# Two graph-attention layers on 128 small graphs: quads of graphs, layer by layer, unrolled, in place of pairs of graphs with both layers interleaved in a loop

## The reference

```python
# layer 0: attention, output projection, residual, norm
q = (x @ Wq + bq).reshape(b, n, H, HD)      # k and v likewise
scores = jnp.einsum('bqhd,bkhd->bhqk', q, k) / jnp.sqrt(jnp.float32(HD))
scores = scores + (1.0 - adj)[None, None, :, :] * -1000000000.0
attn = jax.nn.softmax(scores, axis=-1)
out = jnp.einsum('bhqk,bkhd->bqhd', attn, v).reshape(b, n, d)
x = _layernorm(x + (out @ Wo + bo))
# layer 1: the same with its own Wq, Wk, Wv, a mask where adj == 0, and no Wo
x = _layernorm(x + attention(x))
```

## Time and profile before

| what | value |
|---|---|
| median of 3 runs | 3196.25 us (3194.61 to 3197.16) |
| the profiled execution, its own time | 3195.59 us |
| its span, first to last instruction | 3193.8 us |
| PE, DVE, ACT, POOL busy | 98%, 63%, 53%, 36% of the span |
| granted TensorE clock, mean | 0.992 |
| HBM read, written | 75.11 MB, 33.55 MB |

### The profile page before, as it was taken

One profiled execution on the slowest core, in us unless ns is written; L12 is line 12 of the kernel. 1 busy time (PEld: TensorE's weight loads), 2 busy tenths in 40 slices (PEclk: granted clock), 3 DMA queues, 4 the chain that ended last, 5 costly groups with the idle time before them and its releaser, 6 DMA issues.

```text
span 3193.8 us, 78685 instructions
## 1 busy us (share of the span) xinstructions
PE 3121.4 (98%) x25100; PEld 2796.6 (88%) x25100; DVE 2007.7 (63%) x7062; ACT 1683.2 (53%) x5773; POOL 1157.1 (36%) x1093
## 2 busy tenths in 40 slices
PE   6999999999999999999999999999999999999994
PEld 6998898898888888988988888889889889888894
DVE  4566666666666666666666665666666666666654
ACT  4555555555555555555555555555555555555552
POOL 1333333333333333333333333333333333333332
PEclk9999999999999999999999999999999999999997
DMA  4333333333333333333333333333333333333332
GB/s 154 77 103 102 89 100 97 98 92 96 104 94 90 102 101 90 101 101 93 93 97 103 95 90 105 98 91 102 101 90 97 98 101 92 94 104 95 91 99 70
DMA packets 346121, 310.45 MB, mean 97 GB/s; under 512 B 38896, under 2 KB 301296, under 8 KB 346096
## 3 DMA queue, kind: packets, MB, share of 16 engines
q1 hardware_dynamic: 344800, 309.48, 36.6%
q10 hardware_dynamic: 1296, 0.67, 0.1%
HBM read 75.11 MB, written 33.55 MB: 34 GB/s over the span
## 4 chain that ended last, share of the span: by engine, by line
PE 80%; DVE 12%; issue 5%; DVEq 1%; DMA 0%; POOL 0%; ACT 0%; SPq 0%; POOLq 0%
PE ps_proj L371 41%; PE ps_proj L380 29%; PE ps_att L415 6%; PE ps_score L403 4%; DVE prob L778 4%; DVE x_res L869 2%; DVE x L809 2%; DVE stats L793 1%; DVE neg_max L778 1%; DVE xt_hi L741 1%; DVE mean_var L796 0%; DVE inv_sum L786 0%; DVEq L1004 0%; DMA prob<-w_q 0%; DVEq L775 0%
## 5 line engine op out<-in xcount | busy, mean ns | idle before, releaser
L1030 POOL TENSOR_TENSOR prob<-prob,inv_sum 128x512 f32<-128x512 f32 x512 | 525.5, 1042 | 1153.4 <-DVE inv_sum L786 1153.4
L597 ACT ACTIVATE prob<-prob,neg_max 128x128 f32<-128x128 f32 x2048 | 792.8, 391 | 261.3 <-DVE neg_max L778 261.2
L371 PE MATMUL ps_proj<-xt_hi,w_hi_q 128*128 128x256 f32 x2048 | 593.7, 290 | 32.3 <-ACT xt_hi L607 14.3
L371 PE MATMUL ps_proj<-xt_hi,w_lo_q 128*128 128x256 f32 x2048 | 580.6, 283 | 0.0
L371 PE MATMUL ps_proj<-xt_lo,w_hi_q 128*128 128x256 f32 x2048 | 580.4, 283 | 0.0
L371 PE MATMUL ps_proj<-xt_hi,w_hi_k 128*128 128x256 f32 x2048 | 579.7, 283 | 0.0
L371 PE MATMUL ps_proj<-xt_lo,w_hi_k 128*128 128x256 f32 x2048 | 579.6, 283 | 0.0
L371 PE MATMUL ps_proj<-xt_hi,w_lo_k 128*128 128x256 f32 x2048 | 579.3, 283 | 0.0
L778 DVE CUSTOM_DVE_ANT_0 prob<-ps_score,mask 128x128 f32<-128x128 f32 x2048 | 459.5, 283 | 16.5 <-PE ps_score L403 4.8
L819 DVE STREAM_TRANSPOSE blocks_t<-prob 128x512 f32<-128x512 f32 x512 | 341.7, 696 | 200.4 <-DMA prob_t<-blocks_t 164.3
L371 PEld LDWEIGHTS ps_proj<-xt_hi,w_hi_q 128*128 128x128 f32 x2048 | 392.7, 192 | 56.8 <-DVE x_res L869 17.8
(11 more groups left out here) (78 smaller groups left out, 4996.6 us busy)
## 6 DMA issues: line engine op xcount, KB each, us to landing
prob_t<-blocks_t SPq DMA_DIRECT2D x1024, 128.0 KB, 2.7
y<-x_feat SPq DMA_DIRECT2D x128, 256.0 KB, 2.6
x_res<-x_tok SPq DMA_DIRECT2D x64, 512.0 KB, 3.6
prob_t<-prob SPq DMA_DIRECT2D x512, 64.0 KB, 2.1
out<-y SPq DMA_DIRECT2D x128, 256.0 KB, 2.0
prob_t<-blocks_t SPq DMA_DIRECT2D x256, 64.0 KB, 2.1
y<-y SPq DMA_DIRECT2D x256, 64.0 KB, 2.1
prob<-w_q SPq DMA_DIRECT2D x2, 512.0 KB, 7.0
```

What stands on the lines that cost most here:

```text
L371: last = pe.matmul(ps_out[:, i * T:(i + 1) * T], wp[:, c, cols], xp[:, c, :], start=(c == 0 and n == 0), stop=(c == NC - 1 and n == 2))
L597: last = act.activation(prob[b][:, i, n, :], prob[b][:, i, n, :], ACT.Exp, bias=neg_max[l][b][:, i, n:n + 1], scale=-1.0, accum_out=row_su ...
L1030: pool.tensor_tensor(prob[b][:, i], prob[b][:, i], inv_sum[l][b][:, i, :].unsqueeze(2).to_broadcast([P, HB, NODES]), ALU.mult).then_inc(no ...
```

## The change

The program becomes layer by layer. A step takes a quad of graphs (QB = 4, T = 512 tokens); steps 0 to 31 are layer 0, steps 32 to 63 layer 1, and step 64 finishes. In a step PE projects quad s and, between these units, finishes the attention of quad s-1. q and k are projected with 512 columns a matmul (`feature_unit`, L307 of the new program); v and Wo stay at 512 (`token_unit`, L315). The bank of each result is one of a ring of four, and the units wait for the bank's reader. Layer 0's result goes to DRAM twice (`store_x1`: as tokens with layer 1's value bias, and as turned blocks) and comes back through `load_res` and `load_raw`. POOL makes all low parts of x. Only four weights lie in SBUF at a time; layer 1's k, q and v replace layer 0's around steps 31 and 32. All 65 steps are written out, with no loop (`all_steps`).

In step s, `lp` is the layer projected and `la` the layer of the quad whose attention is finished. In the code s - G counts layer 1's quads, with G = 32.

```diff
-GB = 2
+QB = 4
...
+        x1_tok = nc.dram_tensor("x1_tok", (G, QB, NODES, D), F32, kind="Internal").ap()
+        x1_feat = nc.dram_tensor("x1_feat", (G, QB, P, BLK, NC * SQ), F32, kind="Internal").ap()
...
-        def steps(eng, phase_a, phase_b, last_steps, between=None):
-
-            for g in range(3):
-                phase_a(g)
-                if g == 0 and between:
-                    between()
-                phase_b(g)
-            with eng.Fori(3, G) as g:
-                phase_a(g)
-                phase_b(g)
-            last_steps()
...
+        def all_steps(eng, step):
+
+            for s in range(2 * G + 1):
+                step(s, s % 2, None if s > LAST else s // G, None if s == 0 else (s - 1) // G)
...
+            def turn_probs(a, b):
+                if a > G:
+                    sp.wait_ge(sum_set, QB * a + b - 3)
+                else:
+                    need(sp, att_done, QB * a + b - 3)
+                sp.wait_ge(turned_set, 2 * (QB * a + b) + 2)
                 for n in range(BLK):
...
+            def store_x1(a, b):
+                sp.wait_ge(x1_turned_set, QB * a + b + 1)
+                to = x1_feat[a, b].rearrange("(f n) r k -> f n r k", n=BLK)
+                for r in range(BLK):
+                    sp.dma_start(to[:, :, r, :],
+                                 x1_turned[b % 2][r * SQ:(r + 1) * SQ, :].rearrange("p (n k) -> p n k", n=BLK)
+                                 ).then_inc(x1_feat_out[b % 2], 16)
+                sp.wait_ge(x1_bias_set, QB * a + b + 1)
+                sp.dma_start(x1_tok[a, b], x1_bias[b % 2][:]).then_inc(x1_tok_out[b % 2], 16)
+
+            def carry_attention(a, b):
+                sp.wait_ge(att_done, QB * a + b + 1)
+                sp.wait_ge(at1_blocks_set, QB * (a - G) + b + 1)
                 for n in range(BLK):
-                    sp.dma_start(at1_turned[b][:, n].rearrange("p c f -> p (c f)"),
-                                 at1_blocks[b][n * SQ:(n + 1) * SQ].rearrange("p (n k) -> p n k", n=BLK)
+                    sp.dma_start(attention_turned(b)[:, n].rearrange("p c f -> p (c f)"),
+                                 x1_bias[b % 2][n * SQ:(n + 1) * SQ].rearrange("p (n k) -> p n k", n=BLK)
                                  ).then_inc(at1_in[b], 16)
...
+                def finished(b):
+                    if la == 0:
+                        store_x1(a, b)
+                    else:
+                        store_y(a, b)
+                    if lp is not None:
+                        load_res(s, b, lp)
...
+                if la is not None:
+                    turn_probs(a, 2)
+                    turn_probs(a, 3)
+                if isinstance(s, int) and s == G - 1:
+                    sp.wait_ge(k_done, NC * G)
+                    for h in range(2):
+                        load_weight("k1", h, w_new[h][:], w_new_in[h])
+                if isinstance(s, int) and s == G:
+
...
+                if la == 1:
+                    carry_attention(a, 0)
+                    carry_attention(a, 1)
+                    finished(0)
+                    finished(1)
+                    carry_attention(a, 2)
+                    carry_attention(a, 3)
+                    finished(2)
+                    finished(3)
+                if la == 0:
+                    for b in range(QB):
+                        finished(b)
...
-            def project_t(l, ps_out, w, chunks, done):
-
-                for i, m in enumerate(chunks):
...
-                        parts = [(w_hi[w], xt_hi[l]), (w_hi[w], xt_lo[l]), (w_lo[w], xt_hi[l])]
-                        for n, (wp, xp) in enumerate(parts):
-                            last = pe.matmul(ps_out[:, i * T:(i + 1) * T], wp[:, c, cols], xp[:, c, :],
...
+            def feature_unit(bank, slot, par, m, done):
+
+                cols = slice(m * P, m * P + P)
                 for c in range(NC):
-                    parts = [(hi(c), w_hi[w]), (hi(c), w_lo[w]), (lo(c), w_hi[w])]
-                    for n, (xp, wp) in enumerate(parts):
-                        last = pe.matmul(ps_out[:, :], xp, wp[:, c, :],
+                    parts = [(w_hi[slot], xt_hi[par]), (w_hi[slot], xt_lo[par]), (w_lo[slot], xt_hi[par])]
+                    for n, (wp, xp) in enumerate(parts):
+                        last = pe.matmul(ring[bank][:], wp[:, c, cols], xp[:, c, :],
...
+            def scores(s, b):
+                pe.wait_ge(q_set, NC * s + NC)
+                pe.wait_ge(k_set, NC * s + NC)
+                need(pe, masked_set, 2 * (QB * s + b) - 2)
...
+            def keys_out(s, m, bank, layer):
+                act.wait_ge(k_done, NC * s + m + 1)
+                need(act, score_done, 2 * QB * s)
+                act.activation(k_all[:, m, :].rearrange("p (b j n) -> p b n j", b=QB, n=SQ),
+                               ring[bank][:].rearrange("p (b n j) -> p b n j", b=QB, j=BLK),
+                               ACT.Identity, bias=bk_col[layer][:, m:m + 1]).then_inc(k_set, 1)
...
+                if la == 0:
+                    pe.wait_ge(k_set, NC * s + 4)
+                    project_out(a, 0, 3)
+                    pe.wait_ge(at_lo_set, QB * a + 1)
+                    project_out(a, 1, 0)
+                    pe.wait_ge(at_lo_set, QB * a + 2)
+                    queries(par, 1, 1)
+                    pe.wait_ge(q_set, NC * s + 1)
+                    attend(a, 2, 2)
+                    pe.wait_ge(sum_set, QB * a + 1)
+                    attend(a, 3, 3)
+                    pe.wait_ge(sum_set, QB * a + 2)
+                    queries(par, 2, 0)
+                    pe.wait_ge(q_set, NC * s + 2)
+                    project_out(a, 2, 1)
+                    project_out(a, 3, 2)
+                    pe.wait_ge(at_lo_set, QB * a + 4)
+                    queries(par, 3, 3)
+                if la == 1:
+                if la == 1:
+                    pe.wait_ge(k_set, NC * s + 4)
+                    queries(par, 1, 3)
+                    pe.wait_ge(scaled_set, QB * al + 1)
+                    attend(a, 2, 0)
+                    pe.wait_ge(scaled_set, QB * al + 2)
+                    attend(a, 3, 1)
+                    pe.wait_ge(q_set, NC * s + 1)
+                    queries(par, 2, 2)
+                    pe.wait_ge(q_set, NC * s + 2)
+                    queries(par, 3, 3)
...
+                scores(s, 0)
...
+                scores(s, 1)
...
+                values(par, 1, 1)
+                scores(s, 2)
+                scores(s, 3)
...
+                elif la == 1:
+                    turn_attention(a, 0)
+                    turn_attention(a, 1)
+                    next_x(2)
+                    next_x(3)
+                    finish_start(0, None)
+                    finish_start(1, None)
+                    finish_end(0)
+                    finish_end(1)
+                    turn_attention(a, 2)
+                    turn_attention(a, 3)
+                    finish_start(2, None)
+                    finish_start(3, None)
+                    finish_end(2)
+                    finish_end(3)
...
+                mask_scores(s, 0, lp)
+                mask_scores(s, 1, lp)
+                invert_sums(s, 0)
+                mask_scores(s, 2, lp)
+                mask_scores(s, 3, lp)
+                turn_blocks(s, 0)
+                invert_sums(s, 1)
+                turn_blocks(s, 1)
+                invert_sums(s, 2)
```

## The result

The changed kernel takes 3213.4 us (median of 5 runs, 3205.3 to 3216.4) against 3195.5 us before: a ratio of 1.0051, with a 95% interval of 1.0037 to 1.0066. It is half a percent slower, where I forecast 3162 us and 1.1% faster.

A forecast was written before the change was run, and what follows sets the result against it. PE's work, laid end to end, bounds the kernel before; in layer 1 the masks' chain adds holes. Sum: 13 + 3 + 3030 + 76 + 5 + 34 = 3161 us of span, 3162 in the metric; range 3085 to 3228.

The forecast's parts named there:

- PE's floor in layer 1: PE's own work in a layer-1 step: 12 units, four attends, four scores and changes of kind, 41.7 us.
- The width's 90 us: PE, q and k units at 512 columns instead of 256: 94.6 us a quad against 97.4, saving 90 us over 32.
- everything else on PE is the same: PE: only the q and k units' 256-column work changes, 46.8 to 44.0 us for four graphs in both layers.
- What bounds layer 1: Layer-1 chain through ACT, DVE, SP and POOL ends in late masks; PE idles 1.5 us before scores 2, 0.9 before scores 3.
- a steady step of layer 1 takes 44.1 us, 2.4 more than PE's work: Layer-1 step: scores wait for masks, so 44.1 us against PE's 41.7; paid in 31 steps, 76 us.
- the 45.2 that the prediction named as a sign of being wrong: Layer-1 step length in us; the forecast called itself wrong if a step passed it.
- 3 us for the half clock at the start: PE at the kernel's start: 3 us remain for the half clock and the first scores' wait.
- the forecast's 76 us: Total cost of PE waiting for masks in the 31 layer-1 steps 33 to 63.
- rival 2: SP's and DVE's steps between attend 1 and masks take longer; break-even 1.1 us a step, 3230 at 2.2; chance 0.24.
- Unrolling: Loop branches cost nothing visible, so no gain from unrolling; a rival had the unrolled program starve an engine, 3230, chance 0.05.
- Hidden work: ACT's copies and exponentials, x casts and layer 1's DRAM trip cost PE nothing; keys' 512-column way out taken as 1.2 us.
- Ends: Start and finish: first PE work at 13 us, late layer-1 q weights 5 us once, tail after the last step 34 us.

The follow-up runs named there:

- Cutting either end of it: Two variants of the changed kernel: layer-1 masks of graphs 0 and 1 before finishes 2 and 3, 3053.8 us; all attention carries before stores and loads, 3060.0 us.
- The filler's steps: Changed kernel plus 12 redundant 512-column matmuls (value unit 2, later overwritten) on PE before scores 2 in each layer-1 step: 3170.9 us.
- masks first: Changed kernel with DVE's masks of graphs 0 and 1 ahead of the finishes of graphs 2 and 3 in layer-1 steps: 3053.8 us.
- the fastest: Changed kernel with masks 0 and 1 first, all four carries first, and layer 1's q weights rounded at the start of step 32: 3041.7 us.

## Why the prediction was wrong

- **PE's work: right to 1.5%; its saving: too low.** Layer 0's steps were put at 52.9 us and took 52.19, with no hole; PE's floor in layer 1 was put at 41.7 and is 41.31. The width's 90 us are 78. But two turns of before are 97.4 us against 93.5 now: 3.9 a quad, 125 us in all, where "everything else on PE is the same" left 90. The unrolling is 13 of the rest by PE's records; what is left, about 34 us, no run takes apart.
- **What bounds layer 1: right in its mechanism.** The chain runs as laid out, hop by hop, and PE waits for the masks before scores 2: 2.3 to 4.2 us (1.5 forecast), and then at most 0.5 before scores 3 (0.9 forecast). Cutting either end of it gives 41.31 and 41.75 us, the floor or nearly.
- **The step that failed** is "a steady step of layer 1 takes 44.1 us, 2.4 more than PE's work". It takes 46.76 in the mean, over the 45.2 that the prediction named as a sign of being wrong. Two terms are in that. First, the chain is 1.1 us longer at the masks of the step shown: SP's eight issues of carries 0 and 1 took 6.05 us in place of 5.0 (start, us), and the second inverse deviation took 0.81 in place of 0.55, twice; against that, the carries began 0.4 us early.

```profile
2169.00 6.05 SPq L223 DMA_DIRECT2D prob_t<-x_bias  x8
```

  This step is not typical in its issues. In half of the 30 steps the eight take under 5.1 us, and the mean is 5.28. In the mean the masks start at 34.96 us, 0.9 late, and the lateness comes behind carry 1: from both slow deviations, and from the last landing of carry 3, which took 3.2 to 3.9 us in place of 2.1 in six steps.

  The filler's steps, 45.35 us with the clock up but for two, say that this part is 45.35 - 44.1 = 1.25 us, 39 us over 31 steps. Second, the prediction let PE go on at full clock behind a hole: it put 3 us for the half clock at the start and nothing for it in layer 1. The clock at half costs 1.4 us a step, 42 us in all, measured by filling the hole.
- **The sum closes.** Steps 1 to 31 were 22 us cheaper than forecast; step 0, 32 and both ends together 3 us cheaper. Layer 1's 30 measured steps 33 to 62 were 2.66 x 30 = 80 us dearer. 3161 - 22 - 3 + 80 = 3216, the profiled span being 3214.6. (Most of the difference is that the forecast's 76 us should read 31 x 2.4 = 74.)
- **The range and the sign.** The break-even of 1.1 us more a step, rival 2's, was passed by 1.6. Its mechanism gives 1.25 of the 2.66 us; with the clock kept up the kernel runs at 3170.9, faster than before. So it is the clock's fall that turned the sign. The time lies inside the range, near its upper end, and that is in part luck: rival 2 set that end, and more than half of the excess comes from the clock, which no rival had.
- **Unrolling** was put at nothing, since PE had no hole at the loop's end. It had a small one elsewhere in every turn: 11 us.
- **Hidden work stayed hidden.** K's way out at 512 strided columns is 1.20 us as taken. The stores to DRAM and the loads from it never stand before PE in layer 0, where it has no hole, though HBM traffic has risen to 142.22 MB read and 100.66 MB written.
- **Ends.** First matmul at 13.3 (13 forecast); step 32 was 7.4 us over (5 forecast); from PE's last projection to the end it is 31.6 us (34 forecast).

## What to carry to other kernels

When one stage of a kernel gives PE less work, lay the shortest chain through all other engines beside it: here copies, in-order issues and statistics had to pass between attend 0 and scores 2, 26 us, and the order on one engine (masks before finishes, or carries before stores) was worth 150 to 160 us, twice the matmuls' width. Price a hole on PE with what it does to the clock, not by its length alone; if it can't be closed, work worth nothing put into it may still gain. When a step gets shorter, ask again which engine's queue the late part of the step before now falls into.

## What the runs showed of the hardware

- Holes of 2.3 to 4.2 us of idle time before scores 2, one in each of steps 33 to 62, went with a fall to 1.2 GHz in 28 of the 30, and cost 1.4 us a step more than their length. In the filled kernel, whose longest hole in a step was under 1 us in 22 of these steps, the clock fell in two.
- A matmul of 512 columns is 0.227 us after the last, two of 256 are 0.24: per pair 13 to 17 ns, over 12 matmuls and their unit's change 0.16 us.
- SP's issue of one of a carry's DMAs is 0.60 us as a rule, but some take 0.8 to 2.9 us: 44 of all 2382 issues before, 90 of 2382 in the unrolled kernel before, 103 of 2830 in the changed one. The row of one line, with min, median and max in ns, from the changed kernel:

```profile
L207 SPq DMA_DIRECT2D prob_t<-turned x1024: 542/603/2878, 53.4 to 3190.7; - x171
```

What makes them long was not tested; the kernels without holes have as many (123 with masks first, 110 in the fastest).
- POOL's inverse deviation on one column took 0.55 us in every case before and up to 0.95 in the changed kernel. There DVE's normalisation (L696) ran beside 128 of the 256, and these took 0.78 to 0.84 us; of the other 128 all but one took 0.55. Before, no normalisation ran beside one, but transposes did, at no cost. The row has min, median and max in ns:

```profile
L820 POOL TENSOR_TENSOR rstd<-var_eps,minus_half x256: 549/786/946, 75.6 to 3210.7; 128x1 f32<-128x1 f32 x128
```
